# All TensorE work of a pair in 64x64 tiles, with one tap of each block built off the diagonal

## What is computed

```python
x = group_norm(x)              # groups of 2 channels, the partner picked by least |cosine|
def deform_conv(x, off, w):    # 9 taps; tap k of pixel p looks at p + (DY, DX)[k] + off[k, p]
    py, px = positions in f32; four corners, bilinear weights, outside the image 0
    cols = sum over corners of x[corner] * weight
    return einsum('nckhw,ock->nohw', cols, w)
off1 = make_offset(conv3x3(x, tm1, b), conv3x3(x, tr1, b))  # 4 + 2 = 6 channels
out = relu(batchnorm(deform_conv(x, off1, dcn1_w)))
off2 = make_offset(conv3x3(out, tm2, b), conv3x3(out, tr2, b))
out = batchnorm(deform_conv(out, off2, dcn2_w))
return relu(out + x)
```

## Time and profile before

| | us |
|---|---|
| median of 3 runs | 448.58 (447.6 to 449.65) |
| the profiled execution | 447.31 |
| its span, first to last instruction | 445.4 |
| TensorE busy, share of the span | 93% |
| ACT, DVE, POOL busy | 72%, 70%, 25% |
| sample (L672), weigh (L649), build (L633) busy | 286.7, 109.6, 72.1 |
| conv_taps (L585), places_of_taps (L595) busy | 18.3, 11.9 |

### The profile page before, as it was taken

How to read it: one execution, slowest core, us unless ns; L and a number is a source line. 1 busy time by engine, 2 the same in 40 slices (tenths; PEclk the granted TensorE clock), 3 DMA queues, 4 the chain that set the end, 5 groups by cost and what they waited for, 6 DMA issues and landing times.

```text
span 445.4 us, 18471 instructions
## 1 busy us (share of the span) xinstructions
PE 415.5 (93%) x7435; PEld 308.0 (69%) x7435; DVE 313.4 (70%) x865; ACT 318.5 (72%) x385; POOL 110.6 (25%) x241
## 2 busy tenths in 40 slices
PE   5978999999999999999988999999999999999970
PEld 4755677777777777777865677777777777777860
DVE  4657977777787777776429877877777777777435
ACT  2536787777887777777726788777877778777735
POOL 6203422222222222208002322222222212210000
PEclk9999999999999999999999999999999999999996
DMA  7202332222211122212000242212222222221005
GB/s 224 69 2 45 55 47 44 48 45 45 45 35 30 35 45 45 46 37 39 3 1 6 54 82 37 36 34 44 45 45 45 44 42 41 43 48 37 3 3 189
DMA packets 59385, 20.72 MB, mean 47 GB/s; under 512 B 51680, under 2 KB 59184, under 8 KB 59344
## 3 DMA queue, kind: packets, MB, share of 16 engines
q1 hardware_dynamic: 54464, 17.75, 19.4%
q0 software_dynamic: 4880, 2.37, 2.2%
HBM read 3.24 MB, written 2.10 MB: 12 GB/s over the span
## 4 chain that ended last, share of the span: by engine, by line
PE 88%; ACT 4%; DVE 4%; DMA 1%; issue 1%; SPq 0%; DVEq 0%; ACTq 0%
PE acc_ps L672 57%; PE z_ps L649 13%; PE build_ps L633 10%; PE side_ps L585 3%; PE side_ps L595 2%; ACT S L454 1%; DMA xs<-in_x 1%; PE side_ps L575 1%; ACT raw L507 1%; DVE bstats L764 1%; PE side_ps L615 1%; PE acc_ps L542 1%; PE build_ps L532 1%; ACT conv_sb L431 0%; ACT Z L447 0%
## 5 line engine op out<-in xcount | busy, mean ns | idle before, releaser
L672 PE MATMUL acc_ps<-S,Z 64*64 64x256 f32 x4608 | 286.7, 376 | 1.1 <-ACT S L454 1.0
L454 ACT ACTIVATE S<-build_ps,minus 128x1024 f32<-128x1024 f32 x192 | 203.7, 1111 | 51.6 <-PE build_ps L633 50.7
L672 PEld LDWEIGHTS acc_ps<-S,Z 64*64 64x64 f32 x4608 | 193.7, 132 | 56.4 <-issue 3.8
L649 PE MATMUL z_ps<-wz,xflat 64*64 64x192 f32 x1536 | 109.6, 331 | 0.1
L895 DVE TENSOR_SCALAR S<-build_ps 128x512 f32<-128x512 f32 x96 | 66.1, 689 | 35.2 <-PE build_ps L633 35.1
L447 ACT ACTIVATE Z<-z_ps 128x768 f32<-128x768 f32 x96 | 77.9, 812 | 5.4 <-PE z_ps L649 5.4
L649 PEld LDWEIGHTS z_ps<-wz,xflat 64*64 64x64 f32 x1536 | 71.3, 132 | 12.5 <-issue 0.5
L265 POOL DMA_DIRECT2D moved<-conv_sb x140 | 70.8, 513 | 20.0 <-POOL conv_sb L354 15.8
L633 PE MATMUL build_ps<-feat_rows,cst 64*64 64x512 f16 x576 | 72.1, 381 | 2.9 <-ACT S L454 1.5
L897 DVE TENSOR_SCALAR S<-build_ps 128x512 f32<-128x512 f32 x96 | 65.3, 680 | 0.0
L902 DVE COPY raw<-acc_ps 128x256 f32 (+1 forms) x32 | 13.6, 424 | 67.2 <-PE acc_ps L672 67.2
(11 more groups left out here) (103 smaller groups left out, 260.7 us busy)
## 6 DMA issues: line engine op xcount, KB each, us to landing
xs<-in_x SPq DMA_DIRECT2D x4, 512.0 KB, 6.4
out<-raw SPq DMA_DIRECT2D x7, 256.0 KB, 2.5
moved<-conv_sb POOLq DMA_DIRECT2D x56, 11.2 KB, 1.7
moved<-conv_sb SPq DMA_DIRECT2D x56, 11.2 KB
moved<-conv_sb POOLq DMA_DIRECT2D x56, 11.3 KB, 1.7
wz<-in_dcn_w POOLq DMA_DIRECT2D x2, 288.0 KB, 4.7
feat_rows<-feats SPq DMA_TRANSPOSE x30, 3.7
moved<-conv_sb SPq DMA_DIRECT2D x28, 12.0 KB
```

Source lines behind the costliest of these rows:

```text
L454: act.activation(S[:, (parity + b) % 2, half, 0:ACT_TAPS, :], build_ps[:, 0:ACT_TAPS, :], ACT.Relu, bias=minus2[:, :], scale=1.0 if half = ...
L649: mm = pe.matmul(z_ps[halves[c], i, h * BLOCK_COLS:(h + 1) * BLOCK_COLS], xflat[parity][halves[i], pixels], wz[halves[i], layer, h, b * BL ...
L672: mm = pe.matmul(acc_ps[halves[i], g, 0:HW], Z[halves[g], slot, i, half, j * C:(j + 1) * C], S[halves[g], slot, half, j, i * HW:(i + 1) * ...
```

## The change

Six things change, and they hang together:

- `conv_taps` has one 64x64 matmul per image, on the diagonal (rows 64i to 64i + 63 to the same output partitions). The 54 tap-and-channel results of image i lie in partitions from 64i on; tap k's twelve rows are now 4 + k + 10 r (`ROW_STEP`), and its weights stand in 64 more columns of `wc`.
- Pixels go by four slices of 64 instead of two halves of 128. `places_of_taps` has eight matmuls of 36 columns on the diagonal instead of four of 72. `place_ps`, `grid` and the spots are ordered (block, slice, tap); a spot's partition tells the image. The number of spots is the same.
- `features` has a sixteenth operation: slot 1 is copied to slot 3.
- `build` makes tap 1 from slot 1 in tile (row half 0, column half 1) and from slot 3 in tile (row half 1, column half 0).
- `sample` reads S in four runs of 64 columns.
- In `conv_taps` and `places_of_taps` an increment of `pe_gate` stands behind the waits.

```diff
-TAP_ROW = [(64 * (k // 5) + TAP_ROWS * (k % 5)) for k in range(TAPS)]
+ROW_STEP = 10
+TAP_ROW = [4 + k for k in range(TAPS)]
-WC_COLS = TAP_ROW[TAPS - 1] + TILE_COLS
+WC_COLS = (TAPS - 1) * TAP_ROWS + TILE_COLS
...
-FEAT_OPS = 15
+FEAT_OPS = 16
...
-        wc = sb("wc", [P, 2, WC_COLS])
+        wc = sb("wc", [P, 2, WC_COLS + C])
...
-        feats = sb("feats", [P, IMAGE_BLOCKS, SLOTS, FEATS], F16)
-        feat_rows = sb("feat_rows", [P, 2, IMAGE_BLOCKS, P], F16)
+        feats = sb("feats", [P, SLICE_BLOCKS, SLOTS, FEATS], F16)
+        feat_rows = sb("feat_rows", [P, 2, SLICE_BLOCKS, P], F16)
...
-                rows = slice(TAP_ROW[k], TAP_ROW[k] + TAP_ROWS)
+                rows = slice(TAP_ROW[k], TAP_ROW[k] + (TAP_ROWS - 1) * ROW_STEP + 1, ROW_STEP)
...
                 wait(pe, feat_step, FEAT_OPS * places_read + 1)
-                for c in range(2):
-                    mm = pe.matmul(side_ps[halves[c], 0, :], wc[:, layer, halves[c]], xpad[parity][:, 1:H + 1, 1:W + 1],
-                                   start=True, stop=True)
+                pe.sem_inc(pe_gate, 1)
+                for i in range(2):
+                    mm = pe.matmul(side_ps[halves[i], 0, :], wc[halves[i], layer, WC_COLS:WC_COLS + C],
+                                   xpad[parity][halves[i], 1:H + 1, 1:W + 1], start=True, stop=True)
...
-                for h in range(HALVES):
-                    for c in range(2):
-                        mm = pe.matmul(place_ps[halves[c], :, h, :], moved[:, h * P + c * C:h * P + (c + 1) * C], combine_taps,
-                                       start=True, stop=True)
+                pe.sem_inc(pe_gate, 1)
+                for n in range(SLICES):
+                    for i in range(2):
+                        mm = pe.matmul(place_ps[halves[i], :, n, :], moved[halves[i], n * C:(n + 1) * C],
+                                       combine_taps[halves[i], :], start=True, stop=True)
...
-                for h in range(HALVES):
-                    mm = pe.matmul(place_ps[:, :, h, :],
-                                   conv_sb[:, h * P:(h + 1) * P], combine, start=True, stop=True)
+                for n in range(SLICES):
+                    for i in range(2):
+                        mm = pe.matmul(place_ps[halves[i], :, n, :], conv_sb[:, n * C:(n + 1) * C],
+                                       combine[:, i * SLICE_PLACES:(i + 1) * SLICE_PLACES], start=True, stop=True)
...
-                for j in (0, 2, 1):
-                    rows = halves[j // 2]
-                    for c in range(2):
-                        mm = pe.matmul(build_ps[halves[c], j, :], masks[j % 2][rows, halves[c]],
-                                       feat_rows[rows, parity, b * 2 * HALVES:(b + 1) * 2 * HALVES, :], start=True, stop=True)
+                for j, r, c in ((0, 0, 0), (0, 0, 1), (2, 1, 0), (2, 1, 1), (1, 0, 1), (1, 1, 0)):
+                    mm = pe.matmul(build_ps[halves[c], j, :], masks[j % 2][halves[r], halves[c]],
+                                   feat_rows[halves[r], parity, b * SLICES:(b + 1) * SLICES, :], start=True, stop=True)
...
-                                           S[halves[g], slot, half, j, i * HW:(i + 1) * HW], start=(b == 0 and n == 0),
+                                           S[halves[g], slot, half, j, :].rearrange(by_image, i=2, q=C)[:, i], start=(b == 0 and n == 0),
...
+                    elif op == 16:
+                        ins = dve.tensor_copy(feats[:, :, SLOTS - 1, :], feats[:, :, 1, :])
```

More of the change, by code:

```diff
@@ L17 @@
 from contextlib import ExitStack
+from itertools import accumulate
 import concourse.bass as bass
@@ L60 @@
 SLOTS = 4
-IMAGE_BLOCKS = BLOCKS * 2 * HALVES
-SPOTS = IMAGE_BLOCKS * BLOCK_TAPS
+SLICES = HW // C
+SLICE_BLOCKS = BLOCKS * SLICES
+SPOTS = SLICE_BLOCKS * BLOCK_TAPS
 PLACES = 4 * SPOTS
-HALF_PLACES = PLACES // HALVES
+SLICE_PLACES = PLACES // SLICES
 PLACE_SCALE = 32.0
@@ L69 @@
 WEIGHT_UNIT = 2.0 / PLACE_SCALE ** 2
-FEAT_OPS = 15
-FEAT_OP_NEEDS = {2: 1, 3: 2, 4: 3, 5: 3, 6: 3, 7: 4, 8: 7, 9: 6, 10: 8, 11: 6, 12: 10, 13: 9, 14: 9, 15: 12}
+FEAT_OPS = 16
+FEAT_OP_NEEDS = {2: 1, 3: 2, 4: 3, 5: 3, 6: 3, 7: 4, 8: 7, 9: 6, 10: 8, 11: 6, 12: 10, 13: 9, 14: 9, 15: 12, 16: 15}
 FIRST_OPS, NEXT_OPS = range(1, 9), range(9, FEAT_OPS + 1)
 BN_OPS = 7
[L76 to L80, removed]
+CONST_SIZES = dict(ident=P, fold=P, combine=2 * SLICE_PLACES, combine_taps=SLICE_PLACES, grid=PLACES, iota=C, edges=2)
+CONST_ENDS = list(accumulate(CONST_SIZES.values()))
+CONSTS = {name: (end - size, end) for (name, size), end in zip(CONST_SIZES.items(), CONST_ENDS)}
+CONST_COLS = CONST_ENDS[-1]
 CODES = 16
@@ L185, in program @@
         taken = feats[:, :, 0:BLOCK_TAPS, :]
-        place_ps = side_ps[:, 1, 0:PLACES].rearrange("p (n h k) -> p n h k", h=HALVES, k=4 * BLOCK_TAPS)
+        place_ps = side_ps[:, 1, 0:PLACES].rearrange("p (n s k) -> p n s k", s=SLICES, k=4 * BLOCK_TAPS)
         halves = (slice(0, C), slice(C, P))
@@ L330, in _ @@
                 pool.dma_start(vec[rows, :], vecs).then_inc(weights_in, 16)
-                at = TAP_ROW[CENTRE] + i * OFFS
-                pool.dma_start(bc_centre[at:at + OFFS, :], conv_b).then_inc(weights_in, 16)
+                at = TAP_ROW[CENTRE] + i * OFFS * ROW_STEP
+                pool.dma_start(bc_centre[at:at + (OFFS - 1) * ROW_STEP + 1:ROW_STEP, :], conv_b).then_inc(weights_in, 16)
                 pool.dma_start(bc[i * OFFS:(i + 1) * OFFS, :], conv_b).then_inc(weights_in, 16)
@@ L574, in conv @@
                         rows = (slice(g * H // 4, (g + 1) * H // 4) if k == TAPS - 1 else slice(0, H))
-                        mm = pe.matmul(side_ps[32 * g:32 * g + 32, 0, rows.start * W:rows.stop * W], wc[:, layer, TAP_ROW[k]:TAP_ROW[k] + TILE_COLS],
+                        mm = pe.matmul(side_ps[32 * g:32 * g + 32, 0, rows.start * W:rows.stop * W], wc[:, layer, k * TAP_ROWS:k * TAP_ROWS + TILE_COLS],
                                        xpad[parity][:, rows.start + dy:rows.stop + dy, dx:dx + W],
@@ L657, in sample @@
                 slot = (parity + b) % 2
+                by_image = "p (n i q) -> p i n q"
                 if b == 0:
@@ L884, in features @@
                                                 row_sign[:, :, a:a + 1].rearrange(by_slot, j=BLOCK_TAPS)
-                                                .broadcast_to([P, IMAGE_BLOCKS, BLOCK_TAPS, 8]), ALU.mult)
+                                                .broadcast_to([P, SLICE_BLOCKS, BLOCK_TAPS, 8]), ALU.mult)
                     elif op == 15:
@@ L989, in shape_constants @@
     put("fold", part[:, None] % C == part[None, :] % C)
-    combine = np.zeros((P, BLOCKS, 2, BLOCK_TAPS, 2, 2), np.float32)
     taps = np.arange(TAPS).reshape(BLOCKS, BLOCK_TAPS, 1)
[L992 to L1009, removed]
+    sums = np.zeros((OFFS, BLOCKS, BLOCK_TAPS, 2, 2), np.float32)
+    for axis in range(2):
+        sums[2 * axis, :, :, axis, :] = taps // 3 - 1
+        sums[2 * axis + 1, :, :, axis, :] = taps % 3 - 1
+        sums[4 + axis, :, :, axis, :] = 1
+    sums = PLACE_SCALE * sums.reshape(OFFS, SLICE_PLACES)
+    combine = np.zeros((P, 2, SLICE_PLACES), np.float32)
+    by_tap = np.zeros((P, SLICE_PLACES), np.float32)
+    for i in range(2):
+        for tile in range(P // TILE_COLS):
+            row = tile * TILE_COLS + i * OFFS
+            combine[row:row + OFFS, i] = sums
+        for row in TAP_ROW:
+            at = row + i * OFFS * ROW_STEP
+            by_tap[at:at + OFFS * ROW_STEP:ROW_STEP] = sums
+    put("combine", combine.reshape(P, -1))
+    put("combine_taps", by_tap)
+    grid = np.zeros((P, BLOCKS, SLICES, BLOCK_TAPS, 2, 2), np.float32)
+    for n in range(SLICES):
+        pixel = n * C + part % C
+        grid[:, :, n, :, 0, :] = (pixel // W)[:, None, None, None]
+        grid[:, :, n, :, 1, :] = (pixel % W)[:, None, None, None]
     grid[:, :, :, :, :, 1] -= 1
@@ L1015, in shape_constants @@
         if k % 3 != 1:
-            edges[row:row + TAP_ROWS, 0 if k % 3 == 2 else 1] = 0
+            edges[row:row + TAP_ROWS * ROW_STEP:ROW_STEP, 0 if k % 3 == 2 else 1] = 0
     put("edges", edges)
@@ L1049 @@
                        for n in (1, 2)], axis=1)
-    conv_w = np.zeros((P, 2, WC_COLS), np.float32)
+    conv_w = np.zeros((P, 2, WC_COLS + C), np.float32)
     for i in range(2):
         for k in range(TAPS):
-            conv_w[i * C:(i + 1) * C, :, TAP_ROW[k] + i * OFFS:TAP_ROW[k] + (i + 1) * OFFS] = taps_w[:, :, k, :]
+            at = k * TAP_ROWS + i * OFFS
+            conv_w[i * C:(i + 1) * C, :, at:at + OFFS] = taps_w[:, :, k, :]
+            at = WC_COLS + TAP_ROW[k] + i * OFFS * ROW_STEP - i * C
+            conv_w[i * C:(i + 1) * C, :, at:at + (OFFS - 1) * ROW_STEP + 1:ROW_STEP] = taps_w[:, :, k, :]
     conv_b = np.stack([np.concatenate([a[f"L1_conv_tm{n}_b"], a[f"L1_conv_tr{n}_b"]]) for n in (1, 2)], axis=1)
```

## The result

| | before | with the change |
|---|---|---|
| median, us | 448.28 (447.6 to 449.65, 4 runs) | **436.86** (436.57 to 436.91, 4 runs) |
| ratio, 95% interval | 1 | 0.974 (0.9716 to 0.9764) |
| profiled execution, its span | 447.31, 445.4 | 436.85, 434.9 |
| from one conv to the next in the loop | 11.96 | 11.46, 11.48 |

A forecast was written before the change was run, and what follows sets the result against it. The prediction took TensorE, busy 93% of the span, to bound the kernel. Its terms, -12.0 - 0.6 - 0.8 + 0.6 = -12.8 us, led to a forecast median of 435.8 us, with a range of 428 to 443.

The forecast's parts named there:

- The pair, -12.0: Twelve full pairs in each layer's loop: each falls from 11.96 to 11.46 us, 24 x 0.50 = -12.0 us.
- a pass of places: Places on the diagonal tiles: weight loads set 0.06 us per pass, eight passes taking 0.47 us.
- the drains: Around conv and places: two drains of the array and the loads behind them take 0.27 us per pair.
- the diagonal total of 11.26: Diagonal tiles' work per pair: 10.36 + 0.43 + 0.47 = 11.26 us, the period if all tiles were free.
- The reason for 11.46 between the bounds: Pair start: off-diagonal builds can be sent about three places passes (0.18 us) from the end, giving 11.46 us.
- Pairs of index 13, -0.3 each: Pairs with places alone: drains go and the lead covers the extra 0.22; 2 x -0.3 = -0.6 us.
- First pairs, -0.4 each: Each layer's first pair: four mode changes go, though ACT partly sets the pace; 2 x -0.4 = -0.8 us.
- The copy on DVE: Added slot 1 to slot 3 copy: 0.4 us, counting at each layer's start; 2 x 0.3 = +0.6 us.
- At nothing: Items booked without cost: the moves, larger conv weights, sampling's four runs of 64 columns, direct places of two pairs per layer.
- Rival A: PSUM writes: two row halves take turns in one bank, making the kernel slower, 472 us; chance 0.07.
- Rival B: Pair start: off-diagonal builds wait until every places matmul has started; no change, 448 us; chance 0.06.
- Rival C: Pair start: ACT's conv copy makes rectify 0.3 us late each pair; half the gain, 443 us; chance 0.09.

The follow-up runs named there:

- e1: The changed kernel with both tap 1 build products back in row half 0, from slot 1; 446.85 us.
- e2: The changed kernel with conv and places back in 128-row tiles, padded with zero weights; 452.99 us.
- e5: The changed kernel with off-diagonal builds issued before places and both acc_ps banks read at once by ACT and DVE; 432.06 us.
- e7: e5 with only slices 0 and 1 of places_of_taps computed, old values used for the other two; 424.97 us.
- e4: The changed kernel with ACT copying acc_ps bank 0 while DVE copies bank 1, TensorE waiting for these copies alone; 434.87 us.
- e3: The changed kernel with the four off-diagonal build products issued between conv and places, the diagonal two after places; 435.60 us.
- again: The changed kernel run once more, unaltered, beside e1 to e3; 436.33 us.
- again2: The changed kernel run once more, unaltered, on another chip beside e4 to e6; 437.69 us.
- e6: The kernel before the change, with both acc_ps banks read at once by ACT and DVE; 447.78 us.

## Why the prediction was right

The size was right to 1 us, the pair to 0.02. The steps, and the stretches of the trace that they forecast (profiled execution of before and of after, layer 1 and layer 2). A pair is measured here from its last sampling record to that of the next; every pair has 144 such records, so the last one can be counted off. (From build to build the ends of a stretch can shift by 0.2 us: at the end of a layer the first build record comes 0.26 us ahead of the old pair's last sampling record with the change, and 0.05 before it.)

| stretch | predicted | measured |
|---|---|---|
| ahead of the first sampling, layer 1 | +0.3 | +0.50 |
| the first pair, from its first sampling | -0.4 each | +0.03, -0.09 |
| 12 full pairs | -6.0 each | -5.61, -4.85 |
| the pair of index 13 | -0.3 each | -0.28, -0.28 |
| the last two pairs | 0 | -0.01, -0.01 |
| between the layers | +0.3 | +0.25 |
| behind the last sampling | 0 | -0.22 |
| sum | -12.8 | -10.6 |

The sum explains the spans (434.9 - 445.4 = -10.5). By the medians it is 436.86 - 448.28 = -11.4, and 436.33 - 447.92 = -11.6 in the run beside e1. The first sampling of layer 1 starts at 36.7 to 38.9 us in the executions of these kernels, so a difference of 1 us between two single executions need not be the change's.

- **The pair, -12.0.** Held: 11.97 became 11.46 or 11.48 us, -0.50. The parts held one by one: conv at two slots, a pass of places at 0.058 us (0.06 taken from the Gram product), the drains together with the overlap that they prevent (e2: 0.70 us; no run parts the two), the diagonal total of 11.26 (e5: 11.25; e7: 11.04 for 11.02), the build total with tap 1 in one row half (e1: 11.89 for 11.90). **The reason for 11.46 between the bounds was half of it.** The step said that the off-diagonal builds wait for the stream, up to three passes from the end. They do: e4 has that limit alone, 11.41. But DVE's reads of `acc_ps` give 11.46 to 11.48 by themselves (e3). The prediction had no wait for `acc_ps` at all, and would have been 0.2 us per pair too low, had it assumed the order of e3. That the pair came out at 11.46 to the second digit is in part luck: the two limits happen to lie 0.05 us apart.
- **Not all full pairs gained it.** Early in each loop pairs are slower (see what stays open). That took 0.4 us from layer 1 and 1.2 from layer 2, the largest miss of the sum.
- **Pairs of index 13, -0.3 each.** Held: 11.53 us became 11.25.
- **First pairs, -0.4 each.** Failed: 13.08 and 12.72 us became 13.11 and 12.63. In again and again2 they took 12.62 to 12.84, and 13.34 and 12.71 in e6, whose edit leaves them alone; a gain of 0.4 in each does not show, one of 0.1 or 0.2 might be there. The stall of the build for S in the first pair is as long as in the earlier trace rows, and sampling now waits longer for ACT's S than it did. TensorE's timeline of the kernel after, then the row of the waits of the kernel before, then that of the kernel after (us in total, times, longest):

```profile
47.00 0.62 PE L637 MATMUL build_ps<-feat_rows,cst 64*64 64x512 f16 x6 [0.75 <-ACT S L456]
```

```profile
PE acc_ps L672 <- ACT S L454: 1.0, 2, 0.5
```

```profile
PE acc_ps L677 <- ACT S L456: 1.7, 2, 0.9
```

  ACT sets the pace there: of what the array saves, 0.35 us per first pair goes into that wait. The prediction named this and still booked half.
- **The copy on DVE.** 273 ns instead of 0.4 us; at a layer's start +0.25 us between the layers, and in layer 1 +0.30 us from the second `places` (L615, now L620) to the first transpose (34.00 - 32.14 and 34.48 - 32.32), as booked. TensorE's wait there grew from 1.4 to 2.0 us over two loads, again 0.3 each.
- **At nothing.** The moves, the gates and the four runs in S cost nothing that shows: a slot of sampling is 0.216 us still. The last pairs of a layer cost nothing either, with tap 1 off the diagonal or not. TensorE waits there for DVE's two reads with all tiles, in both kernels: ahead of a pair's first sampling its weight loads stand for 0.35 us in the kernel before (206.86) and 0.33 in the kernel after (201.47). The 0.22 us behind the last sampling are not the change's by what shows: e6, without it, has 0.16 of them.
- **Rival A** (one bank, one row half at a time) fell: products in one bank with different partitions start together, 0.22 us after the two before them, and take 0.38 us as these do (151.18 x2), and the pair is 11.46 us for its 12.95. **Rival B** (starts in program order) fell: 150.93 before 150.96, conv beside sampling. **Rival C** (ACT late at the start): rectify follows the conv copy directly (155.45 + 0.48 = 155.93, about the start of its row), so it was as even as worked out, and the pair shows no cost.

What stays open are the early pairs of the loops. In the kernel after, the pair of index 1 took 11.88 us in layer 1, and those of indices 1 to 4 in layer 2 took 12.01, 11.89, 11.50 and 11.69, where the others took 11.42 to 11.48; before, all twelve took 11.97 in both layers. The slow ones came again: again and again2 have 11.85 and 11.90 at index 1 of layer 1, 12.01 and 11.89 at indices 1 and 2 of layer 2. In each of these executions TensorE's weight loads stand still once in the pair of index 2 of layer 2, for 0.53 us and for no wait that the profile shows. The timeline of the loads, kernel after:

```profile
263.23 0.39 PEld L677 LDWEIGHTS acc_ps<-S,Z 64*64 64x64 f32 x7
264.15 0.54 PEld L677 LDWEIGHTS acc_ps<-S,Z 64*64 64x64 f32 x12 [0.53 <-issue]
```

e3 has the same stop (0.52 us), e4 and e5 have one of 0.29 and 0.57 late in layer 2 instead; the kernel before, e1, e2 and e6, which lack one half of the change or both, have none in their loops but ahead of conv or places. That is a correlation. An obvious suspect is the loading of code: seven packets of the instruction queue q8 land between 248 and 286 us, and none from there to 378. But the kernel before has as many there (seven between 248 and 291 us) and loses nothing, seven land between 49 and 86 us as well, where one pair alone is late, and the stops of e4 (366.92) and e5 (359.48) come long after. No run told the cause.

## What to carry to other kernels

Where a kernel works in 64x64 tiles, count the slots of each of the four tiles separately. Here the count of the fullest tile gave the pair where nothing else held it (11.90 for 11.89 in e1, 11.26 for 11.24 and 11.25 in e5), and moving one product per block to the tiles that are idle during a small step made room for that step, while either half of the move alone was worth next to nothing (11.89 in e1, 12.16 in e2, for 11.96 before). When such a step shrinks, look for what it had covered: the reads of the accumulator cost nothing before (e6), 0.05 us a pair after (e4), and 0.2 once the builds no longer waited as well (e3 to e5). Two limits at the same time hid each other here (11.46 or 11.48 us in e3, 11.41 in e4, 11.24 and 11.25 with both edits in e5), so an edit without a gain (e3) is worth trying together with the next (e5).

## What was unexpected of the hardware

- Two tiles write different partitions of one PSUM bank at the same time at the full pace: both records of 151.18 start together, a slot (0.22 us) after the two of 150.96, and take 0.38 us as these do.
- It was the stream of instructions that stood, and not the array, when the off-diagonal tiles idled 0.38 us: sent first, their builds start one slot, 0.22 us, after the last sampling record (153.46, 153.68 in e3).
- Leaving 64x64 tiles for conv and places cost 0.70 us per pair in e2 (12.16 - 11.46), though each diagonal tile has the same slots and passes for them as with the change. The drains and the lost overlap were not told apart.
- Stops of the weight loads of 0.5 us in the loop of layer 2 (263.62 to 264.15), without a releaser in the trace, at the same pair in three executions of one kernel.
